# The last stage's pair loop in another order: next pair's work between gates, down-product and quantisation

## The reference, cut to what matters

```python
x = x + L1_ffn(y)                    # y: attention's output, two halves to be summed
#   base = y @ W_up.T; top1 = argmax(y @ gate_w.T + bias) of 4
#   base + one_hot(top1) x (lora_B (lora_A y)), rank 8
x = x + L2_ffn(L2_cond(x))
#   c = x @ W + (x A[idx]) B[idx], 16 adapters, one per sequence, rank 16
#   h = silu(c w1' + c a1' b1'/2) * (c w3' + c a3' b3'/2), 1376 wide, w tiled 4 times
#   h w2' (tiled) + (h a2') b2'/2
x = x + L3_ffn(L3_cond(x))
#   c3 = x @ W.T + 2 * sum over the top 2 of 8 experts (language bias 5.0), rank 16
#   amax = max|c3| per token; q = clip(round(c3 / (amax/127))); q @ qweight (int8)
#   result * amax/127 * wscale + bias
```

## Time and profile before

| | us |
|---|---|
| median of 3 runs | 3247.13 (3244.84 to 3252.37) |
| profiled execution | 3248.76 |
| its span, first to last instruction | 3246.8 |
| PE busy in the span | 3034.6 (93%) |
| DVE busy | 1556.9 (48%) |
| ACT busy | 1293.1 (40%) |
| POOL busy | 1532.6 (47%) |

### The profile page before, as it was taken

How to read it: one execution, slowest core, us unless ns; L and a number is a source line. 1 busy time by engine, 2 the same in 40 slices (tenths; PEclk the granted TensorE clock), 3 DMA queues, 4 the chain that set the end, 5 groups by cost and what they waited for, 6 DMA issues and landing times. The chain is left out here.

```text
span 3246.8 us, 55910 instructions
## 1 busy us (share of the span) xinstructions
PE 3034.6 (93%) x15256; PEld 2022.1 (62%) x15264; DVE 1556.9 (48%) x3931; ACT 1293.1 (40%) x3014; POOL 1532.6 (47%) x1323
## 2 busy tenths in 40 slices
PE   3799999999999999999999999999999986888887
PEld 2466666666666666666666666666666664555454
DVE  6544444444444444444444444444444444556555
ACT  1344444444444444444444444444444431222221
POOL 7355555555555555555555555555555520001000
PEclk9899999999999999999999999999999997999898
DMA  8544444434443444545444444344444443112110
GB/s 294 192 122 123 117 117 117 118 117 118 117 118 117 118 118 125 189 123 176 124 119 120 119 120 121 118 127 123 126 118 123 123 148 100 31 37 53 32 30 13
DMA packets 416196, 378.26 MB, mean 117 GB/s; under 512 B 83427, under 2 KB 347763, under 8 KB 414996
## 3 DMA queue, kind: packets, MB, share of 16 engines
q1 hardware_dynamic: 358484, 186.81, 20.2%
q0 software_dynamic: 50480, 174.40, 17.2%
q10 hardware_dynamic: 7056, 14.46, 1.2%
HBM read 341.23 MB, written 25.85 MB: 113 GB/s over the span
## 5 line engine op out<-in xcount | busy, mean ns | idle before, releaser
L533 DVE CUSTOM_DVE_ANT_0 ps_s<-ps_s,mask 128x544 f32<-128x544 f32 x512 | 374.9, 732 | 938.8 <-PE ps_s L360 929.2
L262 POOL DMA_INDIRECT v_sb<-in_v_rows_w,v_row x504 | 488.3, 969 | 469.3 <-PE ps_oT L385 258.7
L319 PE MATMUL ps_t<-wqkv,xT 128*128 128x512 f32 x1488 | 704.1, 596 | 0.0
L383 PEld LDWEIGHTS ps_oT<-pT,v_sb 128*128 128x128 f32 x4096 | 527.0, 192 | 186.6 <-issue 186.1
L433 ACT ACTIVATE ps_s<-ps_s,nmax 128x544 f32<-128x544 f32 x512 | 352.3, 688 | 628.9 <-DVE nmax L533 627.8
L383 PE MATMUL ps_oT<-pT,v_sb 128*128 128x128 f32 x4096 | 541.3, 275 | 9.8 <-issue 9.8
L343 PE MATMUL ps_t<-wo,oT 128*128 128x512 f32 x1024 | 524.8, 597 | 2.5 <-ACT oT L448 0.9
L359 PE MATMUL ps_s<-k_sb,qT 128*128 128x416 f32 x1024 | 446.9, 518 | 19.2 <-issue 15.2
L543 DVE TENSOR_SCALAR p_sb<-ps_s,rinv 128x544 f32<-128x544 f32 x512 | 401.3, 784 | 23.9 <-DVE rinv L540 0.3
L448 ACT ACTIVATE oT<-ps_oT 128x128 f32<-128x128 f32 x512 | 141.9, 277 | 637.0 <-PE ps_oT L385 634.3
L368 PEld LDWEIGHTS ps_pT<-ident_sb,p_sb 128*128 128x128 f32 x2048 | 251.3, 141 | 188.3 <-issue 185.4
(11 more groups left out here) (216 smaller groups left out, 3775.4 us busy)
## 6 DMA issues: line engine op xcount, KB each, us to landing
k_sb<-in_kT SPq DMA_DIRECT2D x2048, 64.0 KB
v_sb<-in_v_rows_w,v_row POOLq DMA_INDIRECT x512
v_new<-v_raw SPq DMA_DIRECT2D x128, 64.0 KB, 3.3
wo<-in_wo_w POOLq DMA_DIRECT2D x2, 4096.0 KB, 15.3
y_scratch<-y_sb SPq DMA_DIRECT2D x32, 256.0 KB, 2.1
xT<-x1T_scratch POOLq DMA_DIRECT2D x31, 256.0 KB, 4.6
tab<-rope_scratch POOLq DMA_DIRECT2D x31, 256.0 KB, 4.7
wqkv<-in_wqkv_w ACTq DMA_DIRECT2D x6, 1024.0 KB, 10.6
```

The costliest lines, as they stand in the source:

```text
L262: e.indirect_dma_start(out=v_sb[:, b % 2, c, :], out_offset=None, in_=A["v_rows_w"], in_offset=bass.IndirectOffsetOnAxis(ap=v_row[:, b, c: ...
L319: m = e.matmul(ps_t[bank_of(t)][:, :], xT[:, k, :], wqkv[:, k, 512 * t:512 * t + 512], start=k == 0, stop=k == KC - 1)
L383: e.matmul(ps_oT[:, :], v_sb[:, b % 2, c, h * D:(h + 1) * D], pT[:, u % 2, c, :], start=c == 0, stop=False)
L533: e.tensor_tensor_reduce(out=scores(u), in0=scores(u), in1=mask[:, b % 2, :], scale=-SCALE, scalar=3e38, op0=ALU.add, op1=ALU.min, accum_o ...
```

## The change

The steps are the same but for one; their order, banks and buffers differ. After the gates of pair k TensorE does the next pair's turn of y's sum, its router product (`gate_logits`) and the up-product of group 0; after b3 the up-product of group 1, delta, the turn of x2 and `states`, and between and behind them the turns and int8 products of pair k, one group at a time. The product for the low-rank inputs moves from `states` to `states_end`, behind the mask. VectorE routes the next pair behind the gate chain, does the next x2 between the two quantisations, the masks beside the rescales, and bias and output in the same pair, ahead of the splits. y is loaded two pairs ahead. The sum of y's halves is turned into a buffer of its own, `aT`. GpSimd has no work left in the stage: its additions go to VectorE, between the gate product and the reductions. Down-product, w3 and int8 product move to bank 3, the up-product to bank 1. Cut to its core (the new helper functions hold the old instructions, with the banks just named):

```diff
@@ sync
+            def load_y(k, p):   # the two y loads, taken out of load
...
+            def body(k, first=False, last=False):
+                if not last:
+                    for p in both:
+                        e.wait_ge(event["c_done"], 2 * k + p + 1)
+                        load(k + 1, p)
+                if not first:
+                    for p in both:
+                        store(k - 1, p)
+                if not last:
+                    for p in both:
+                        e.wait_ge(event["a_turned"], 2 * (k + 1) + p + 1)
+                        if not (isinstance(k, int) and k == I_STEPS - 2):
+                            load_y(k + 2, p)
@@ tensor
+            def turn_a(k, p):
+                if not first(k):
+                    e.wait_ge(silued, 8 * (k - 1) + 4 + p + 1)
+                turn4(k, p, a, "a_sum", "a_turned")
+            def gate_logits(k, p):
+                e.wait_ge(event["a_copied"], 2 * k + p + 1)
+                if not first(k):
+                    e.wait_ge(silued, 8 * (k - 1) + 6 + p + 1)
+                product(p, gz, E1 + E1 * R1, 2, aT).then_inc(event["z_done"], 1)
+            def up(k, p):
+                if not first(k):
+                    e.wait_ge(multiplied, 8 * (k - 1) + 4 + p + 1)
+                product(p, wup, HID, 1, aT, stop=False)
...
+            def states(k, p):
+                e.wait_ge(event["x2_copied"], 2 * k + p + 1)
+                e.wait_ge(dma_ab[p], 16 * 2 * GB * (k + 1))
+                for c in range(KC):
+                    m = e.matmul(bank[p][2][0:GB * R2, 0:P], A2g[p][:, c, :], xT[p][:, c, :], start=c == 0, stop=c == KC - 1)
+                m.then_inc(event["xr_done"], 1)
+                for c in range(KC):
+                    e.matmul(bank[p][1][:, 0:P], w2f[:, c, 0:P], xT[p][:, c, :], start=c == 0, stop=False)
+            def states_end(k):
+                for p in both:
+                    e.wait_ge(event["xr_masked"], 2 * k + p + 1)
                     for c in range(KC):
+                        e.matmul(bank[p][2][0:TR, P:2 * P], w2f[:, c, P:FOLDED], xT[p][:, c, :], start=c == 0, stop=False)
+                    e.matmul(bank[p][2][0:TR, P:2 * P], B2g[p][:, P:FOLDED], xrm[p][:, :], start=False, stop=True).then_inc(event["t_done"], 1)
                     e.matmul(bank[p][1][:, 0:P], B2g[p][:, 0:P], xrm[p][:, :], start=False, stop=True).then_inc(event["c_done"], 1)
...
                         if j == 0:
                             e.wait_ge(event["c_copied"], 2 * k + p + 1)
+                        if j == 1 and not first(k):
+                            e.wait_ge(event["d_scaled"], 2 * (k - 1) + p + 1)
...
+            def body(k, more=True):
+                gates(k)
                 if more:
+                    for p in both:
+                        turn_a(k + 1, p)
+                    for p in both:
+                        gate_logits(k + 1, p)
+                    up(k + 1, 0)
+                down(k, more)          # down-product to b3; waits for z_masked of k + 1 before the router
+                if more:
+                    up(k + 1, 1)
+                    delta(k + 1)       # z turned, its product, x2 turned
+                    states(k + 1, 0)
+                quantised(k, 0)        # turn of c_qb
+                if more:
+                    states(k + 1, 1)
+                last_product(k, 0)
+                quantised(k, 1)
+                if more:
+                    states_end(k + 1)
+                last_product(k, 1)
@@ scalar
+            def body(k, more=True):
...                                        # the eight Silus
+                if more:
+                    turned_a(k + 1)
...                                        # usT, x3T, exp, gT, cc
+                if more:
+                    turned_z(k + 1)        # zmT, xT of x2
+                for p in both:
+                    quantised(k, p)
+                if more:
+                    state(k + 1)
@@ gpsimd
-        @block.gpsimd
-        def _(e):
-            with e.Fori(0, I_STEPS) as k:
-                for j in range(1, 4):
-                    for p in range(2):
-                        e.wait_ge(multiplied, 8 * k + 2 * j + p + 1)
-                        if j > 1:
-                            e.wait_ge(chunk_summed, 4 * k + 2 * (j - 2) + p + 1)
-                        e.tensor_tensor(us[p][:, 0:HC], ...
@@ vector, in the gate chain
                         e.wait_ge(multiplied, n)
                         if j:
+                            if j > 1:
+                                e.wait_ge(chunk_summed, 4 * k + 2 * (j - 2) + p + 1)
+                            e.tensor_tensor(us[p][:, 0:HC], us[p][:, 0:HC] if j > 1 else u[p][:, 0:HC], u[p][:, at],
+                                            ALU.add).then_inc(chunk_summed if j < 3 else event["u_summed"], 1)
                             e.wait_ge(low_ranked, n - 2)
...
+            def body(k, more=True):
+                done[0] = HEAD + CH * k
+                gate(k)
                 if more:
                     route(k + 1)
+                third(k)                   # x3, experts' choice, hg
+                if more and not (isinstance(k, int) and k == I_STEPS - 2):
+                    sum_halves(k + 2)
+                quantise(k, 0)
+                if more:
+                    second(k + 1, 0)       # x2
+                    second(k + 1, 1)
+                quantise(k, 1)
+                if more:
+                    mask_states(k + 1, 0)
+                rescale(k, 0)
+                if more:
+                    mask_states(k + 1, 1)
+                output(k, 0)
+                rescale(k, 1)
+                output(k, 1)
+                if more:
+                    for p in both:
+                        split_low_rank(k + 1, p)
```

More of the change, by code:

```diff
@@ L1140, in turn4, with product, delta @@
                 m.then_inc(event[done], 1)
-            def product(k, p, weights, n, b, start=True, stop=True, lhs=xT):
+            def product(p, weights, n, b, lhs, start=True, stop=True, at=0):
                 for c in range(KC):
-                    m = e.matmul(bank[p][b][:, 0:n], lhs[p][:, c, :], weights[:, c, :], start=start and c == 0, stop=stop and c == KC - 1)
+                    m = e.matmul(bank[p][b][:, at:at + n], lhs[p][:, c, :], weights[:, c, :], start=start and c == 0, stop=stop and c == KC - 1)
                 return m
[L1147 to L1158, removed]
+            def turn_a(k, p):
[11 more added lines that the diff above has]
+                product(p, wup, HID, 1, aT, stop=False)
+            def delta(k):
                 for p in both:
@@ L1163, in rest @@
                     e.wait_ge(event["z_copied"], 2 * k + p + 1)
[L1164 to L1165 removed]
+                    e.matmul(bank[p][1][:, :], zmT[p][:, :], lb1[:, :], start=False, stop=True).then_inc(event["delta"], 1)
+                if first(k):
                     e.wait_ge(dma_w, REST)
@@ L1198, in rest, with down @@
                         m.then_inc(gated, 1)
+            def down(k, more):
                 for p in both:
@@ L1234, in _ @@
+                quantised(k, 0)
[6 more added lines that the diff above has]
+                last_product(k, 1)
+            first = lambda k: isinstance(k, int) and k == 0
             e.wait_ge(dma_beside, 16 * len(BESIDE))
             e.wait_ge(padded, 1)
-            head(0)
-            rest(0, start=True)
+            for p in both:
+                turn_a(0, p)
@@ L1238, in _ @@
+            for p in both:
+                gate_logits(0, p)
+                up(0, p)
+            delta(0)
+            for p in both:
+                states(0, p)
+            states_end(0)
+            body(0)
             with e.Fori(1, I_STEPS - 1) as k:
-                rest(k)
-            rest(I_STEPS - 1, more=False)
+                body(k)
+            body(I_STEPS - 1, more=False)
         @block.scalar
@@ L1246, in copy, with turned_a, turned_z @@
                 e.activation(to, of, func, **more).then_inc(event[done], 1)
-            both = (0, 1)
-            def head(k):
+            def turned_a(k):
                 for p in both:
-                    copy(k, p, xT[p][:, :, :], four(bank[p][0]), "a_turned", "a_copied")
-            def rest(k, more=True):
+                    copy(k, p, aT[p][:, :, :], four(bank[p][0]), "a_turned", "a_copied")
+            def turned_z(k):
                 for p in both:
@@ L1443, in split @@
                 e.tensor_copy(parts[:, :], b[0:TR, :]).then_inc(setup, 1)
+            sum_halves(0)
             split(b1x, b1s)
-            sum_halves(0)
+            route(0)
             split(b3x, b3s)
-            route(0)
-            rest(0, start=True)
+            for p in both:
+                second(0, p)
+            e.wait_ge(dma_w, REST)
+            e.tensor_copy(langf[:, :], langi[:, :]).then_inc(setup, 1)
```

(17 more changed lines are left out.)

188 lines of the change are left out of this document (86 added, 102 removed).

## The result

| | before | after |
|---|---|---|
| median | 3245.99 (3241.43 to 3252.37, 4 runs) | 3195.45 (3189.22 to 3198.38, 4 runs) |
| profiled span | 3246.8 | 3193.8 |
| PE busy | 3034.6 (93%) | 3024.6 (95%) |
| DVE busy | 1556.9 | 1552.8 |
| POOL busy | 1532.6 | 1490.8 |

The ratio is 0.984 (95% interval 0.9818 to 0.9863): 50.5 us faster. The kernel with the change is 3.5 us above the forecast of 3192.

What follows compares the result with a forecast made beforehand. No engine is full; dependences bound the pair, in turns of two engines. Span 2721.5 + 55.8 (pair 0) + 355.5 (pairs 1 to 6) + 58.9 (pair 7) = 3191.7, as a median about 3192 us; own range 3180 to 3202.

Steps and rivals of the forecast that it cites:

- (1): Second half of a pair, first b3 matmul to next gates: 18.2 us instead of 25.1, 6.9 saved.
- (2): VectorE's splits come late behind the old pair's output: its first gate multiply 3.0 us later after the gates' start.
- (3): VectorE's gate chain with the additions moved there: unit 2.16 us, chain 16.1 instead of 17.3, 1.2 saved.
- (4): First half, gates' start to first b3 matmul: 41.0 us, before 41.5; pair 59.2, saved 7.4.
- (5): The ends of the stage: pair 0 55.8 us, first gates at 2721.5, pair 7 net unchanged at 58.9.
- my bounds of 0 and +3: Prologue before the first gates: change in us from the weights' landing and new y loads, taken as 0.
- rival A: Clock falls in TensorE's new 3.1 to 3.2 us gap before the first bf16 gate product; 3210 us, chance 0.19.
- The prediction's own sign of being wrong: At the gates: 0.50 in the clock behind the new gap would show that the clock falls there.
- two units late come to 2.3 to 2.8 us a pair: Cost of gates starting at 1.2 GHz, at 2.9 us a unit, over seven pairs; gives 3210 us.
- B: Gate chain's first reduction stays at 1.15 us without GpSimd; 25 us over eight pairs, 3217 us, chance 0.08.
- C: Splits not so late, without any of the 3.8 us of wait: 55.5 us a pair, 3170 us, chance 0.07.
- D: TensorE runs through the body's wide products at 1.2 GHz; 3276 us with 12 us a pair, chance 0.05.

Runs made afterwards that it cites:

- Splits first: Against the changed kernel, VectorE does the next pair's two splits before rescale and output of group 1; 3166.66 us, 0.9775 of before.
- output late: Changed kernel with next pair's splits before group 1's rescale, and its bias and output behind the next gate chain; 3156.99 us, 0.9749 of before.
- head late: Changed kernel with next pair's turns, logits, routing and both up-products put behind b3 again; 3269.32 us, 1.0086 of before.
- old tail: Changed kernel with the order of before restored behind b3 (both quantisations, both last products, then delta, x2, states, splits); 3192.38 us, 0.9853 of before.

## Why the prediction was right

The order did what the prediction says, and its steps come out within 0.7 us each. It failed at one place, the clock in the new gap (last paragraphs of this section). The steps against pair 3, whose clock doesn't fall (2895.46 to 2954.68, 59.22 us).

(1) The second half, 18.2 forecast, is 18.25 (2936.43 to 2954.68). VectorE waits for delta between the two quantisations as foreseen (rows of pair 4's second half):

```profile
3001.79 0.43 DVE L1491 TENSOR_SCALAR c_qb<-c_qf 128x512 bf16<-128x512 f32 x1
3004.15 1.45 DVE L1418 TENSOR_TENSOR c_x<-c_x,c_ps 128x512 f32<-128x512 f32 x2 [1.94 <-PE c_ps L1196]
```

(2) Late splits: first bf16 gate product 4.35 after the gates' start forecast, 4.27 measured; first multiply 6.1 and 6.3. Splits first and output late show the price, 2.5 us a pair, and with the output moved too 3.4.

(3) The unit of the gate chain, 2.16 forecast, is 2.07, and the chain some 15.4 instead of 16.1. The 0.72 from multiply to reduction held a wait for the multiply's end, of which the row of before shows 0.22; in the new unit the multiply is followed by the addition after 0.65. The reductions are both 0.57, or 0.50 from start to start as forecast, which is the term I was least sure of; with the additions back on GpSimd the first is 1.23. The Trainium skill's statement ("GPSIMD Engine Reference", Key points) that VectorE instructions with two SBUF inputs contend with GpSimd agrees with both traces.

(4) The first half, 41.0 forecast, is 40.97; down-product at 22.88 (23.0), 5.42 us (5.2).

(5) Pair 0 is 55.64 (55.8), pair 7 58.8 (58.9). The first gates at 2718.7, not 2721.5, mostly the 2.1 us of the shared part; the other 0.7 us is a shorter prologue, on the far side of my bounds of 0 and +3. Two slips in the working change nothing: six pairs of 59.2 are 355.2, not 355.5, and twice 1.95 is 3.9, not 3.8.

Where it failed: rival A came true, to which I had given 0.19, and its price was wrong. The prediction's own sign of being wrong showed, 0.50 in the clock behind that gap. In the four pairs 1, 2, 4 and 6 the clock fell, so the six pairs took 360.6 instead of 355.5. The term that was mis-sized is "two units late come to 2.3 to 2.8 us a pair": it is 1.3, and it fell due in four pairs, not in seven (pair 7 fell too and paid nothing). At 1.2 GHz for 3.4 us TensorE loses 1.7 us. Of that 0.16 is a wait that it has at full clock (before group 1's bf16 product, at 2901.52) and not at half; the other 0.2 I can't place. The gates end 16.4 us after their start instead of 15.1 and nothing waits from there to the down-product, so the 1.3 us go on whole. I had argued from VectorE's chain, which ends 0.5 us later only. My argument against A, that a 3.25 us gap of before had stayed at 1.00, was no argument. The clock fell in gaps of 2.94 us. The stretch that I had read ends at 3234, 0.3 us after that gap; in the same trace the clock falls at 3235.7, and in the change the fall came up to 1.3 us after a gap's end. And the same gap in pair 7 of the change, before the turn of the quantised group, fell too (0.61 against 0.40 in the earlier trace rows):

```profile
3182.60 0.61 PE L1166 MATMUL c_ps<-c_identb,c_qb 128*128 128x128 bf16 x4 [3.25 <-DVE c_qb L1491]
```

That the span came within 2.1 us of its forecast is in part luck: the 5.1 us of clock, which I had left to the rival, met 2.8 us of earlier first gates, 2.1 of them the shared part that the change doesn't touch. The Trainium skill ("TensorE: Matmul & The Clock Gate", Part 1), with the throttled state as the default, bears on it: the traces agree in 18 of the 28 gaps of this kind in four profiles (the change's two, additions back on GpSimd, head late) and disagree in ten. B fell (reductions 0.57), C fell (59.2, not 55.5), and D fell: in the change's two profiles the clock came back each time after 3.4 us, in the gates themselves. The run with GpSimd's additions shows that this isn't certain, with one fall of 6.8 us, but there too it came back in the gates.

## What to carry to other kernels

Fill the hole in which one engine waits for the other's chain with work of the next iteration: it gives back the hole and the slow clock behind it. Then look at once at what stands in the other engine's queue before the first thing that the next iteration needs; here results of the old iteration (bias, output) stood before the splits, and moving them was worth another 29 us in the body, some 5 of them the clock. A reordering of two halves should be tried by halves, since one of them can be paying for the other.

## What the runs showed of the hardware

A gap of 2.92 to 2.95 us on TensorE behind the same work took the clock to 1.2 GHz in 18 cases of 28, in four profiles, and not in the other ten; why not in these stays open. With the gap filled down to 0.63 us it fell in none of seven. In the old tail a gap of 2.90 us did it in three pairs of seven. At the gates 17 falls lasted 3.4 us and one 6.8. A 344-wide reduction with two SBUF inputs takes 0.57 us alone and 1.14 to 1.23 beside a 0.91 us GpSimd addition, so the addition on GpSimd cost VectorE 0.57 to 0.66 us, more than the 0.43 that it costs VectorE to do it itself.
